# Third norm's units over four PSUM banks, low transposes ahead of the averages, a table load moved and bias preparation on GpSimd, in a fused cross-attention kernel

## What is computed

```python
def _cross_attention(q_in, kv_in, wq, bq, wk, bk, wv, bv, wo, bo, bias_k, bias_v):
    qh = (q_in @ wq + bq).reshape(b, q_len, H, K)
    kh = concatenate([(kv_in @ wk + bk).reshape(b, t, H, K), bias_k])   # one more token
    vh = concatenate([(kv_in @ wv + bv).reshape(b, t, H, K), bias_v])
    weights = softmax(einsum('bqhk,bthk->bhqt', qh, kh) / sqrt(K))
    return einsum('bhqt,bthk->bqhk', weights, vh).reshape(b, q_len, H * K) @ wo + bo
x = x + _cross_attention(_layer_norm(x), ctx, ...)        # layer 0
x = x + _cross_attention(_layer_norm(x), ctx, ...)        # layer 1
x = x + gelu(_layer_norm(x) @ w_fc1 + b_fc1) @ w_fc2 + b_fc2
a = _layer_norm(ctx)
Q, K, V = x @ Wq.T, a @ Wk.T, a @ Wv.T                    # 16 heads of 16
out = x + tanh(gate) * (softmax(Q K.T * scale, mask) V) @ Wo.T
```

## Time and profile before

| | us |
|---|---|
| median of 3 runs | 1471.31 (1470.87 to 1472.1) |
| the profiled execution | 1475.24, of which 1473.2 are its span |
| PE busy | 1417.8 (96%) |
| DVE busy | 985.8 (67%) |
| ACT busy | 868.5 (59%) |
| POOL busy | 471.0 (32%) |
| mean granted clock of TensorE | 0.994 |

### The profile page before, as it was taken

How to read it: one execution, slowest core, us unless ns; L and a number is a source line. 1 busy time by engine, 2 the same in 40 slices (tenths; PEclk the granted TensorE clock), 3 DMA queues, 4 the chain that set the end, 5 groups by cost and what they waited for, 6 DMA issues and landing times.

```text
span 1473.2 us, 24729 instructions
## 1 busy us (share of the span) xinstructions
PE 1417.8 (96%) x9188; PEld 891.8 (61%) x9188; DVE 985.8 (67%) x2034; ACT 868.5 (59%) x1566; POOL 471.0 (32%) x379
## 2 busy tenths in 40 slices
PE   9999999999999899999999999999999999999987
PEld 5466666666666554466666666666554454555545
DVE  6765555555555557766666566665556888888886
ACT  5744554455445447555445544554445788889896
POOL 3545334334334200234432523420011333334300
PEclk9999999999999999999999999999999999999999
DMA  6299899888888730599989989887722799999998
GB/s 207 78 227 192 164 183 184 175 173 179 179 172 182 150 97 29 115 207 182 190 161 185 182 165 181 179 165 147 180 51 50 136 210 211 220 214 223 215 199 164
DMA packets 672083, 246.95 MB, mean 168 GB/s; under 512 B 644716, under 2 KB 646236, under 8 KB 671964
## 3 DMA queue, kind: packets, MB, share of 16 engines
q1 hardware_dynamic: 671964, 245.38, 82.4%
HBM read 85.28 MB, written 0.52 MB: 58 GB/s over the span
## 4 chain that ended last, share of the span: by engine, by line
PE 71%; DVE 9%; ACT 7%; DMA 6%; issue 3%; SPq 2%; ACTq 0%; DVEq 0%
PE SC L769 38%; PE PV L769 33%; DMA core<-qc 3%; DVE qc L1556 2%; ACT qc L1295 2%; DVE core L1597 2%; DMA core<-core 2%; DVE prob L1538 2%; DMA qc<-core 2%; ACT prob L1286 1%; ACT core L1279 1%; ACT small L1303 1%; DVE core L1589 1%; SPq L515 1%; SPq L557 0%
## 5 line engine op out<-in xcount | busy, mean ns | idle before, releaser
L769 PE MATMUL PV<-core 128*128 128x256 f16 (+1 forms) x4800 | 540.5, 270 | 17.3 <-DMA core<-qc 5.6
L769 PEld LDWEIGHTS PV<-core 128*128 128x128 f16 x4800 | 458.4, 98 | 87.5 <-issue 13.7
L1228 ACT ACTIVATE prob<-SC,core 128x500 f32<-128x500 f32 x336 | 223.7, 674 | 413.0 <-DVE core L1562 413.0
L769 PE MATMUL SC<-ctxT,qc 128*128 128x500 f16 x2016 | 443.7, 374 | 0.0
L1531 DVE TENSOR_REDUCE mx<-SC 128x1 f32<-128x500 f32 x336 | 224.4, 669 | 322.5 <-PE SC L769 322.5
L769 PEld LDWEIGHTS SC<-ctxT,qc 128*128 128x128 f16 x2016 | 196.0, 97 | 206.8
L697 POOL CAST ctxT<-stage 128x750 f16<-128x750 f32 x64 | 68.9, 1076 | 446.7 <-PE SC L769 235.5
L1589 DVE SCALAR_TENSOR_TENSOR core<-prob,core 128x1500 f16<-128x1500 f32 x112 | 194.6, 1738 | 4.1 <-ACT core L1237 4.0
L1237 ACT ACTIVATE core<-prob 128x1500 f16<-128x1500 f32 x112 | 162.7, 1453 | 3.5
L769 PE MATMUL SC<-ctxT 128*128 128x512 f16 x576 | 136.9, 381 | 9.1 <-DVE core L1597 8.9
L769 PE MATMUL SC<-qc 128*128 128x512 f16 x480 | 112.7, 379 | 13.0 <-DVE mx L1538 13.0
(11 more groups left out here) (134 smaller groups left out, 1329.0 us busy)
## 6 DMA issues: line engine op xcount, KB each, us to landing
stage<-in_ctx_nat_dram SPq DMA_DIRECT2D x64, 384.0 KB, 4.0
stage<-in_ctx_t_dram SPq DMA_DIRECT2D x64, 375.0 KB, 3.4
stage<-in_ctx_p_dram SPq DMA_DIRECT2D x32, 384.0 KB, 3.9
core<-in_wq_dram SPq DMA_DIRECT2D x8, 512.0 KB, 4.0
core<-in_wk_dram SPq DMA_DIRECT2D x8, 512.0 KB, 3.6
core<-in_wv_dram SPq DMA_DIRECT2D x8, 512.0 KB, 5.2
core<-in_wo_dram SPq DMA_DIRECT2D x8, 512.0 KB, 5.0
core<-core SPq DMA_TRANSPOSE x224, 4.2
```

Of the source, the lines that this page charges most:

```text
L769: return nc.tensor.matmul(o, a, c, start=start, stop=stop, skip_group_check=skip)
L1228: nc.scalar.activation(prob[:, i, c * CW:c * CW + w], SETS[i][c][:, 0:w], ACT.Exp, bias=nmax[:, i, :], accum_out=sum3[:, i, c:c + 1]).then ...
```

## The change

Four edits.

1. `unit_bank`: units 0 to 7 go over four banks in turn (M, S[1], PV[0], PV[1]) and not two. PE waits from unit 4 on for the unit four back (`m_lo`, n - 3), where it waited from unit 2 on for the unit two back. Units 8 and later keep the two banks. The MLP's first output product, which writes PV[0], gets a wait for `m_lo` 8.
2. In SP's attention list, at step 56, the last low transpose (L515) stands ahead of the transpose of average 53 (L523), where it stood behind it.
3. The load of the square root's activation table on ACT stands behind the copy of the turned token column, and no longer at the top of the output projection.
4. All bias preparation but one small subtraction goes from DVE to POOL, ahead of POOL's spread. DVE keeps the low rows of `bvd16`, in step 2 of attention 0. DVE's wait for `in_pack` moves into `fill(1)`; ACT's is gone. The first weights' halves are handed out anew: high (2, 3) from `fill(1)` to `fill(2)`; low (0, 1) and (2, 3) become (0), (1) and (2, 3).

```diff
         def unit_bank(n, y):
+            if n < FIRST_MLP_UNIT:
+                return (M, S[1], PV[0][:, :], PV[1][:, :])[n % 4]
             if n < PRE_UNITS:
                 return (M, S[1])[n % 2]
...
                     if 1 <= x <= TILES:
                         turn_high(t0 + x - 1)
-                    if 1 <= x < TILES:
+                    if 1 <= x <= TILES:
                         turn_low(t0 + x - 1)
...
                         turn_average(t0 + x - LAG - 1)
-                    if x == TILES:
-                        turn_low(t0 + x - 1)
...
+            pool.wait_ge(in_pack, 32)
+            for l in range(2):
+                for n in ("bq", "bv"):
+                    v = pk[:, PACK[n, l]:PACK[n, l] + H]
+                    ins = nc.gpsimd.tensor_scalar(v, v, W_SCALE, None, ALU.mult)
+            ins.then_inc(bq_scaled, 1)
+            for l in range(2):
+                a, c = PACK["bias_k", l], PACK["bk", l]
+                nc.gpsimd.tensor_tensor(bkd[:, l, :], pk[:, a:a + H], pk[:, c:c + H], ALU.subtract)
+            nc.gpsimd.tensor_tensor(bvd[:, :, :], vr[:, :, 0, :], vr[:, :, 1, :], ALU.subtract).then_inc(bd_step, 1)
+            pool.wait_ge(bd_step, 1)
+            nc.gpsimd.tensor_scalar(bkd[:, :, :], bkd[:, :, :], W_SCALE, None, ALU.mult)
+            nc.gpsimd.tensor_scalar(bvd[:, :, :], bvd[:, :, :], W_SCALE / TOK_SCALE, None, ALU.mult).then_inc(bd_step, 1)
+            pool.wait_ge(bd_step, 2)
+            nc.gpsimd.tensor_copy(bkd16[:, :, 0, :], bkd[:, :, :])
+            nc.gpsimd.tensor_copy(bvd16[:, :, :], bvd[:, :, :]).then_inc(bd_step, 1)
+            pool.wait_ge(bd_step, 3)
+            nc.gpsimd.tensor_tensor(bkd16[:, :, 1, :], bkd[:, :, :], bkd16[:, :, 0, :], ALU.subtract).then_inc(bkd_ready, 1)
             pool.wait_ge(bkd_ready, 1)
...
-                if n < PRE_UNITS and n >= 2:
+                if 4 <= n < FIRST_MLP_UNIT:
+                    pe.wait_ge(m_lo, n - 3)
+                if FIRST_MLP_UNIT <= n < PRE_UNITS:
                     pe.wait_ge(m_lo, n - 1)
...
+                    if f == 0:
+                        pe.wait_ge(m_lo, FIRST_MLP_UNIT)
...
                         nc.scalar.activation(tokT, TB[0][0:TILES, 0:P], ACT.Copy).then_inc(tok_moved, 1)
+                        table(ACT.Sqrt)
...
             def output_projection(l):
-                table(ACT.Sqrt)
...
-            act.wait_ge(in_pack, 32)
-            layer_norm(0, lambda at: [weights_high(2 * W_Q[0] + i) for i in ((0, 1), (2, 3), ())[at]])
+            layer_norm(0, lambda at: [weights_high(2 * W_Q[0] + i) for i in ((0, 1), (), (2, 3))[at]])
...
+                    if x == LAG and l == 0:
+                        r = TOK_ROWS[1]
+                        dve.wait_ge(bd_step, 3)
+                        nc.vector.tensor_tensor(bvd16[r:r + H, :, :], bvd[r:r + H, :, :], bvd16[r:r + H, :, :],
+                                                ALU.subtract).then_inc(bvd_ready, 1)
...
-            dve.wait_ge(in_pack, 32)
...
             def first_fill(at):
-                for i in ((0, 1), (2, 3), ())[at]:
-                    weights_low(2 * W_Q[0] + i)
...
+                if at < 2:
+                    weights_low(2 * W_Q[0] + at)
+                    if at == 1:
+                        dve.wait_ge(in_pack, 32)
+                else:
+                    for i in (2, 3):
+                        weights_low(2 * W_Q[0] + i)
```

More of the change, by code:

```diff
@@ L1696, in audio_attention @@
                         mask_term_of(b + 1)
-            dve.wait_ge(in_pack, 32)
-            for l in range(2):
-                a, c = PACK["bias_k", l], PACK["bk", l]
-                ins = nc.vector.tensor_tensor(bkd[:, l, :], pk[:, a:a + H], pk[:, c:c + H], ALU.subtract)
-            nc.vector.tensor_tensor(bvd[:, :, :], vr[:, :, 0, :], vr[:, :, 1, :], ALU.subtract).then_inc(bd_step, 1)
-            dve.wait_ge(bd_step, 1)
-            nc.vector.tensor_scalar(bkd16[:, :, 0, :], bkd[:, :, :], W_SCALE, None, ALU.mult)
-            nc.vector.tensor_scalar(bvd16[:, :, :], bvd[:, :, :], W_SCALE / TOK_SCALE, None, ALU.mult)\
-                .then_inc(bd_step, 1)
-            dve.wait_ge(bd_step, 2)
-            nc.vector.scalar_tensor_tensor(bkd16[:, :, 1, :], bkd[:, :, :], W_SCALE, bkd16[:, :, 0, :],
-                                           ALU.mult, ALU.subtract).then_inc(bkd_ready, 1)
-            r = TOK_ROWS[1]
-            nc.vector.scalar_tensor_tensor(bvd16[r:r + H, :, :], bvd[r:r + H, :, :], W_SCALE / TOK_SCALE,
-                                           bvd16[r:r + H, :, :], ALU.mult, ALU.subtract).then_inc(bvd_ready, 1)
-            def first_fill(at):
-                for i in ((0, 1), (2, 3), ())[at]:
-                    weights_low(2 * W_Q[0] + i)
-                if at == 1:
-                    for l in range(2):
-                        for n in ("bq", "bv"):
-                            v = pk[:, PACK[n, l]:PACK[n, l] + H]
-                            ins = nc.vector.tensor_scalar(v, v, W_SCALE, None, ALU.mult)
-                    ins.then_inc(bq_scaled, 1)
+            def first_fill(at):
+                if at < 2:
[5 more added lines that the diff above has]
+                        weights_low(2 * W_Q[0] + i)
             layer_norm(0, first_fill)
```

## The result

| | before | after |
|---|---|---|
| median of the runs made together | 1471.7 us (4 runs, 1470.87 to 1474.78) | 1461.14 us (4 runs, 1460.06 to 1462.09) |
| ratio | | 0.9923 (0.9909 to 0.9938) |
| the profiled execution, span in it | 1475.24, 1473.2 | 1462.04, 1460.3 |
| mean granted clock | 0.994 | 0.998 |

The change saves 10.6 us between the medians (9.1 to 13.4 by the interval), and 13.2 between the profiled executions; 14.3 were forecast. Nine more runs of the kernel before and four of the changed one, on another chip, gave 0.9914 (0.9900 to 0.9927). The time lies in the range, the direction is right, and the forecast of 1457.0 is 4.1 us too low.

What follows compares the result with a forecast made beforehand. PE, busy 96% of the span, was taken as the bound, gaining by seam waits or its clock; 2.4 + 4.0 + 2.6 + 5.3 = 14.3 us off the median gave 1457.0 us, range 1455.0 to 1462.5.

Steps and rivals of the forecast that it cites:

- Start: Up to layer 0's first product: earlier subtraction, earlier spread and full clock gain 2.4 us, bounds 1.0 and 2.9.
- The 0.3 for GpSimd keeping DVE out: At the start: a GpSimd operation delays DVE's low half of the first weight, 0.3 us taken off the gain.
- Tail 0: Tail of attention 0: PE's wait for token rows shrinks by 2.4 us, clock gives 1.6; 4.0 us, bounds 1.5 and 4.2.
- Tail 1: Tail of attention 1: table load leaves the path, 1.3 us, clock gives 1.3; 2.6 us, bounds 1.1 and 2.9.
- a seam takes nothing: Rival: token rows arrive late or the MLP hands back the third norm's gain; 3 to 4 us less, 1460.5; 10 in 100.
- Third norm: Mean to first output product: four banks save waits of 0.9 + 3.0, clock 1.7, less 0.4; 5.3 us, bounds 3.2 and 5.5.
- The new wait that I put at 0.4: In the third norm, PE waits 0.4 us before unit 8 for DVE's units 5 and 6.
- The clock: Full clock at the start and after shortened waits: 1.6 us at tail 0, 1.3 at tail 1, 1.7 in the third norm.
- the clock still falls: Rival: clock drops at most seams despite shorter gaps; waits alone save 8.7 us, 1462.6; two or more falls stay, 20 in 100.

Runs made afterwards that it cites:

- the halves alone: The kernel before with only the handing out of the first weights' halves as changed, bias preparation still on DVE; 1471.1 us.
- the two experiments with a filler: The kernel before with eight constant matmuls ahead of `token_value(0)`, 1468.02 us; the changed kernel with early weight loads and two constant matmuls in the token wait, 1458.58 us.
- two edits taken apart: The kernel before with the last low transpose ahead of the average's, 1476.23 us; the kernel before with the table load behind the turned column's copy, 1469.43 us.

## Why the prediction was right, and what in it was off

**Start.** Forecast 2.4 us. The first two profiles differ by 3.49 at the first product and 2.54 after attention 0, and 0.6 of the 3.49 are the mean's matmuls, by luck. All profiles give the forecast: the first product comes at 16.21 in the mean of eight without edit 4 (the halves alone left out) and at 13.70 in the mean of five with it, 2.5 us, and at the turned column of attention 0 it is 497.79 and 495.28, 2.5 again. So what attention 0 takes back in the ledger (0.95) is not seen in the mean and not put down to the change. The 0.3 for GpSimd keeping DVE out was not paid, since it is GpSimd that pays. DVE's low half at 8.31 takes its usual 0.69, and GpSimd's cast beside it is the one that is stretched. GpSimd, the changed kernel and then its repeat, where no low half is beside the cast:

```profile
8.39 0.69 POOL L678 CAST core<-core 128x32 f16<-128x32 f32 x1
```

```profile
8.75 0.21 POOL L678 CAST core<-core 128x32 f16<-128x32 f32 x1
```

In the profile of edit 4 alone DVE paid once as well: two low halves at 13.06 took 1.52 us and not 1.28, beside a GpSimd select. And GpSimd was stretched there too, where the low half of 8.68 meets another operation of GpSimd (0.85 in the changed kernel):

```profile
8.79 1.29 POOL L676 TENSOR_SCALAR core<-core 128x256 f32<-128x256 f32 x1
```

The Trainium skill, "SBUF — State Buffer", "Who interferes with whom", calls the port pair that the two engines share an exclusive lock, and has the order of issue decide who is blocked. The rows agree: the low half had started first both times (8.31 before 8.39, 8.68 before 8.79), and GpSimd lost 0.4 to 0.5 us, off the path.

**Tail 0.** Forecast 2.4 of wait and 1.6 of clock; the ledger has 2.6 to 2.8 and 1.38. The chain was right link by link: transpose 495.5 less the shift, table load out of the way, rows early, 0.7 us left. But the 2.4 was mis-sized: it was read from the one profile whose tail 0 was 1 us dearer than in the five others, and against those the change saves 1.6. The clock's 1.38 was there to be saved in five profiles of six, 1.15 in the mean.

**Tail 1.** Forecast 1.3 and 1.3; measured 1.47 and 1.35, wait 0.69 for 0.85. The fall came in three profiles of six, so 0.7 in the mean. Here the step that failed is not in the tail but right behind: the sum let the 2.6 us run through to the third norm, though the weights of output projection 1 are issued behind the last average and four loads. 0.94 us went there in the changed kernel (1.14 in its repeat), 4.0 in the profile of edits 2 and 3 alone. The rival "a seam takes nothing" had the mechanism (a gain handed to another wait) and the wrong place.

**Third norm.** Forecast 5.3, measured 5.39, and 5.38 with edit 1 alone. The new wait that I put at 0.4 is not there. Against two profiles without edit 1 in which no fall came here (23.15 us from mean to first output product, and 19.45 with edit 1) it is 3.7; with a fall in seven of nine, 5.0 in the mean.

**The clock.** The forecast holds 5.6 us of it (14.3 less the 8.7 of the rival that saves waits alone). The mean clock of the runs gives 5.6 against nine runs of before and 6.2 against twenty-nine. So the size was right: the falls counted over the profiles make 5.9 us at the four seams in the mean, 2.3 at the start, 1.4 and 0.9 at the tails, 1.3 in the third norm. My reading was right only in part. "Waits of 2.15, 2.73 and 2.99 us were each followed by the half clock" was true of one profile; a second profile had 2.46 and 2.15 without a fall, and another kernel 3.00 without one. A long gap costs its fall in 22 of 29 cases and not in each; behind a shortened one there was none in 26. So a seam's price has to be multiplied by its odds, 5 in 6 at tail 0 and 3 in 6 at tail 1. The falls at places that no edit touches stay: the changed kernel's own profile fell in the second norm. The rival "the clock still falls" (1462.6) is out: no fall at the four seams, and 3.3 us left of the clock's part and not 8.8.

**The sum and the base.** Of the 8.7 us of waits some 7.3 came (12.8 less 5.6; 5.8 by the twenty-nine: 1473.07 less 1461.11, the mean of the first four runs after, less 6.2). The losses have names: 0.8 of tail 0's wait (1.6 for 2.4) and 0.94 in output projection 1 make 1.7. Added up by the means over all profiles, the terms are 2.5 at the start, 2.7 at tail 0, 1.2 at tail 1 and 5.0 in the third norm, 11.4 us; the means of the runs are 12.0 to 12.8 apart. The other miss is the base: I took the median of three runs, 1471.31, as the kernel's time. The kernel before makes 1472.86 over 29 runs (1470.3 to 1477.41) and 1473.3 over nine. So 1.6 to 2.0 us of the 4.1 are the base, and the rest is the sum, 12.4 for 14.3. From the profiled execution the forecast was 1460.9, and the profiled execution after is 1462.04: off by 1.1, but that profile had the dear tail 0 and a fall at all four seams, so this is luck. What is not settled: attention 1's DMA wait near 620 us, 1.94 here, 1.14 in the kernel before and 0.43 and 0.44 in the two experiments with a filler; and the swing of the audio attention.

## What to carry to other kernels

Follow a gain past its seam to the next transfer whose issue doesn't move with it: here 512 KB of weights queued behind four loads took back 0.9 to 1.1 us, and 4.0 in one profile; issuing them first ends that wait, though in the whole change it is not shown in the time. Price a clock fall by rows at both levels, but multiply it by how often it comes, which one profile can't tell; several profiles and the mean clock of several runs can. Read a wait from more than one profile too: tail 0 was 1 us dearer in the first than in five others, and two edits taken apart against it seemed to add up where each alone was worth little. Where several things end one behind the other, an edit to one is worth only the distance to the next. And a median of three runs is no base for a sum whose terms are 2 us.

## What the runs showed of the hardware that was not expected

The granted clock after one and the same wait: 0.76 in one profile and 1.00 in the next, at 2.1 to 2.7 us; 0.79 and 1.00 after 3.0 us. Over fourteen profiles 22 of 29 long gaps were followed by a fall and none of 26 short or filled ones, a wait of 1.60 us among these; a fall took 1.7 us. Small GpSimd operations are cheap, 0.23 us for 128x16 and 0.85 for 128x256 in float32, and beside a low half of DVE it was GpSimd that was held up, by 0.4 to 0.5 us. An activation table load took 1.28 us wherever it stood, and cost nothing off the path. A load of 512 KB behind four others was waited for 2.67 us, although its issue itself takes 0.43.
